# Cross-attention in two blocks of 128 rows on one core: the softmax maxima enter the transposed scores by a 16-row matmul instead of by a DMA into the stacked operand, and the value products are issued four heads at a time

## The reference

```
x = x + L0_xattn(layernorm(x), ctx, ctx)        # this change
x = x + L0_ffn(layernorm(x))                    # one expert product, top-k gates
x = x + L1_xattn(layernorm(x), ctx, mask)
x = x + L1_ffn(layernorm(x))                    # half of the rows, 256 -> 1024 -> 256

def L0_xattn(q, k, v):                          # q, k, v: (16, 128, 256); 8 heads of 16 channels
    qh, kh, vh = (t.reshape(16 * 8, 16, 256) for t in (q, k, v))
    qk = einsum('bdm,bdn->bmn', qh, kh) / sqrt(16)
    return einsum('bmn,bcn->bcm', softmax(qk), vh).reshape(16, 128, 256)
```

## Time and profile before

| what | value |
|---|---|
| time, median of 3 runs | 532.57 us (530.19 to 534.9) |
| span of the profiled execution | 531.3 us |
| PE / DVE / ACT / POOL busy | 361.3 (68%) / 318.5 (60%) / 170.0 (32%) / 94.2 (18%) us |
| DMA moved | 32.87 MB, 62 GB/s in the mean |

### The profile page before, as it was taken

The page is one execution under the profiler, slowest core; times in us unless marked ns, Lnnn a source line. Parts: engine busy times, 40 slices in busy tenths (PEclk is TensorE's granted clock), DMA queues, the critical chain, the costliest instruction groups (busy, mean ns, idle before and its releaser), DMA issues.

```text
span 531.3 us, 7624 instructions
## 1 busy us (share of the span) xinstructions
PE 361.3 (68%) x1872; PEld 207.4 (39%) x1872; DVE 318.5 (60%) x989; ACT 170.0 (32%) x397; POOL 94.2 (18%) x222
## 2 busy tenths in 40 slices
PE   0023494796795795796696799952002699999996
PEld 0011241242342342242243344420002488888885
DVE  6625154376475376376276377546886678887841
ACT  3200151252352252252252344420000125555531
POOL 1101021131131131131130011010001233333310
PEclk9999998699798799699699799985555559999999
DMA  3634363062062062063042000071000000000001
GB/s 104 164 110 103 89 160 74 8 167 68 6 163 71 4 161 72 5 159 73 7 122 73 4 22 1 2 260 57 0 1 0 1 1 11 30 20 20 20 21 41
DMA packets 23763, 32.87 MB, mean 62 GB/s; under 512 B 3466, under 2 KB 21818, under 8 KB 22202
## 3 DMA queue, kind: packets, MB, share of 16 engines
q1 hardware_dynamic: 23706, 32.58, 22.8%
q10 hardware_dynamic: 32, 0.01, 0.0%
HBM read 24.02 MB, written 8.39 MB: 61 GB/s over the span
## 4 chain that ended last, share of the span: by engine, by line
PE 40%; DMA 25%; DVE 15%; issue 7%; SPq 6%; POOL 3%; ACT 2%; DVEq 0%; POOLq 0%; ACTq 0%
DMA q_stack<-neg_max 17%; PE pv_bank L1042 14%; PE t_bank L1248 4%; PE pv_bank L1166 4%; DMA q_parts_dram<-q_parts 4%; PE scoret_bank L1028 4%; DMA q_stack<-q_parts_dram 3%; PE score_bank L1015 3%; SPq L238 3%; PE t_bank L1070 2%; PE score_bank L1229 2%; DMA x_stage<-in_x_dram 1%; PE score_bank L1196 1%; DVE junk L669 1%; DVE equal L669 1%
## 5 line engine op out<-in xcount | busy, mean ns | idle before, releaser
L518 DVE TENSOR_REDUCE row_max<-score_bank 128x2 f32<-128x512 f32 x112 | 75.9, 679 | 121.9 <-PE score_bank L1015 121.7
L1042 PE MATMUL pv_bank<-probs,values_ones 128*32 128x256 f32 x512 | 143.1, 407 | 0.0
L859 ACT ACTIVATE probs<-scoret_bank 128x512 f32<-128x512 f32 x128 | 74.2, 591 | 124.9 <-PE scoret_bank L1028 123.8
L1028 PE MATMUL scoret_bank<-q_stack,k_stack 98*128 98x256 bf16 (+1 forms) x256 | 52.6, 289 | 65.9 <-DMA q_stack<-neg_max 62.9
L1042 PEld LDWEIGHTS pv_bank<-probs,values_ones 128*32 128x32 f32 x512 | 47.7, 114 | 59.0 <-issue 32.5
L1015 PE MATMUL score_bank<-k_stack,q_stack 96*128 (+1 forms) x240 | 49.7, 294 | 24.6 <-DMA q_stack<-q_parts_dram 24.6
L1028 PEld LDWEIGHTS scoret_bank<-q_stack,k_stack 98*128 98x128 bf16 (+1 forms) x256 | 24.7, 102 | 78.3 <-issue 70.1
L358 POOL TENSOR_SCALAR var_eps<-mv 128x1 f32<-128x1 f32 x48 | 9.1, 190 | 192.1 <-DVE mv L554 108.8
L1015 PEld LDWEIGHTS score_bank<-k_stack,q_stack 96*128 (+1 forms) x240 | 17.0, 100 | 66.9 <-issue 27.5
L1166 PE MATMUL pv_bank<-q_stack,k_stack 128*128 (+1 forms) x256 | 36.1, 285 | 0.4 <-ACT q_stack L991 0.4
L1166 PEld LDWEIGHTS pv_bank<-q_stack,k_stack 128*128 128x128 f32 x256 | 33.8, 201 | 1.3 <-issue 0.9
(11 more groups left out here) (182 smaller groups left out, 539.7 us busy)
## 6 DMA issues: line engine op xcount, KB each, us to landing
k_parts_dram<-k_parts SPq DMA_DIRECT2D x24, 128.0 KB
q_parts_dram<-q_parts SPq DMA_DIRECT2D x24, 128.0 KB
k_stack<-k_parts_dram SPq DMA_DIRECT2D x8, 384.0 KB
q_stack<-q_parts_dram SPq DMA_DIRECT2D x8, 384.0 KB
ctx_stage<-in_ctx_dram SPq DMA_DIRECT2D x8, 256.0 KB, 3.2
x_stage<-in_x_dram SPq DMA_DIRECT2D x8, 256.0 KB, 4.2
k_stack<-k_parts_dram SPq DMA_DIRECT2D x8, 256.0 KB
q_stack<-q_parts_dram SPq DMA_DIRECT2D x8, 256.0 KB
```

The costliest lines, as they stand in the source:

```text
L518: dve.tensor_reduce(row_max[:, i, :, h], score_bank[h % 2][:, :].rearrange("p (m n) -> p m n", m=2), AX.X, ALU.max).then_inc(s["max_done"], 1)
L859: act.activation(probs[:, j % 4, :], scoret_bank[j % 2][:, :], ACT.Exp).then_inc(s["exp_done"], 1)
L1028: ins = pe.matmul(scoret_bank[j % 2][:, k * D:(k + 1) * D], k_stack[0:SROWS, slot, h, b_in, k * P:(k + 1) * P], q_stack[0:SROWS, slot, h, ...
L1042: ins = pe.matmul(pv_bank[i][pair * Q:(pair + 1) * Q, odd * D:(odd + 1) * D], values_ones[:, i, k, pair, odd, :], probs[:, j % 4, k * D:(k ...
```

## The change

1. The rows 96 and 97 of the stacks are gone, with the DMA that filled the ones and all `load_neg_max` transfers. Instead DVE negates and splits the maxima before they are transposed (`split_max`, two instructions on 128 x 16 elements in place of one on 8 x 256), one bf16 transpose a half brings both parts of 8 heads to 16 partitions, ACT copies them (`take_neg`) to `neg_rows` (16 x 512), and each half of `scores_t` becomes two matmuls: the 96-row product, and on top of it 16 rows of `neg_rows` against `head_ones`, a constant which is one in the two rows of the head. The semaphore `neg_done` takes the place of `neg_loaded`.
2. The heads are taken in the order 0 2 4 6 1 3 5 7, `probs` has 8 slots, and `values` is called at every fourth step only, for four heads, whose 32-column outputs lie in four different partition groups.
3. `taken_out` and `pick_t`, used in the last layer, lie in a slot of `k_stack`; four small DVE instructions early on make `head_ones`.

```diff
-            def load_neg_max(u, i):
-                wait_apart(sp, s["neg_done"], 2 * u + i + 1)
-                for part in range(2):
-                    sp.dma_start(q_stack[QROWS + part:QROWS + part + 1, u % SLOTS, :, i, :],
-                                 neg_max[:, i, part, :]).then_inc(neg_loaded[i], 16)
...
-            def neg_low(b, i):
+            def split_max(b, i, reused):
+                if reused:
+                    dve.wait_ge(s["max_t"], b - 1)
+                dve.wait_ge(s["max_done"], NH * (b + 1))
+                dve.tensor_scalar(neg_parts[:, i, :, 0, :], row_max[:, i, :, :], -1.0, None,
+                                  ALU.mult).then_inc(s["neg_hi"], 1)
                 dve.wait_ge(s["neg_hi"], b + 1)
-                dve.scalar_tensor_tensor(neg_max[:, i, 1, :], t0_bank[0:NH, 0:D], -1.0, neg_max[:, i, 0, :],
-                                         ALU.mult, ALU.subtract).then_inc(s["neg_done"], 1)
+                dve.scalar_tensor_tensor(neg_parts[:, i, :, 1, :], row_max[:, i, :, :], -1.0, neg_parts[:, i, :, 0, :],
+                                         ALU.mult, ALU.subtract).then_inc(s["neg_split"], 1)
...
+            def take_neg(b, i):
                 act.wait_ge(s["max_t"], b + 1)
-                act.mul(neg_max[:, i, 0, :], t0_bank[0:NH, 0:D], -1.0).then_inc(s["neg_hi"], 1)
+                act.copy(neg_rows[:, i, :], neg_psum).then_inc(s["neg_done"], 1)
...
                 for k in range(2):
-                    ins = pe.matmul(scoret_bank[j % 2][:, k * D:(k + 1) * D],
-                                    k_stack[0:SROWS, slot, h, b_in, k * P:(k + 1) * P],
-                                    q_stack[0:SROWS, slot, h, b_in, :], start=True, stop=True)
+                    pe.matmul(scoret_bank[j % 2][:, k * D:(k + 1) * D],
+                              k_stack[0:QROWS, slot, HEADS[h], b_in, k * P:(k + 1) * P],
+                              q_stack[0:QROWS, slot, HEADS[h], b_in, :], start=True, stop=False)
+                    ins = pe.matmul(scoret_bank[j % 2][:, k * D:(k + 1) * D], head_ones[:, h, :],
+                                    neg_rows[:, b_in, :], start=False, stop=True)
...
-                pe.wait_ge(s["exp_done"], t + 1)
-                pair, odd = h // 2, h % 2
+                pe.wait_ge(s["exp_done"], t + GROUP)
                 for k in range(2):
-                    ins = pe.matmul(pv_bank[i][pair * Q:(pair + 1) * Q, odd * D:(odd + 1) * D],
-                                    values_ones[:, i, k, pair, odd, :], probs[:, j % 4, k * D:(k + 1) * D],
-                                    start=(k == 0), stop=(k == 1))
+                    for pair in range(GROUP):
+                        ins = pe.matmul(pv_bank[i][pair * Q:(pair + 1) * Q, odd * D:(odd + 1) * D],
+                                        values_ones[:, i, k, pair, odd, :],
+                                        probs[:, GROUP * odd + pair, k * D:(k + 1) * D],
+                                        start=(k == 0), stop=(k == 1))
...
-                    values(STEPS * u + j, 2 * u + j // NH, j, first)
+                    if j % GROUP == GROUP - 1:
+                        values(STEPS * u + j + 1 - GROUP, 2 * u + j // NH, j + 1 - GROUP, first)
```

More of the change, by code:

```diff
@@ L31 @@
 QROWS = 6 * C
-SROWS = QROWS + 2
+NR = 2 * NH
+GROUP = NH // 2
+HEADS = [0, 2, 4, 6, 1, 3, 5, 7]
 DIGITS = 15
@@ L78, in build_program @@
         row_max = sb("row_max", [P, 2, 2, NH])
-        neg_max = sb("neg_max", [NH, 2, 2, D], BF16)
+        neg_parts = sb("neg_parts", [P, 2, 2, 2, NH], BF16)
+        neg_rows = sb("neg_rows", [NR, 2, D], BF16)
+        part_head = sb("part_head", [P, 1])
+        head_is = sb("head_is", [P, NH])
+        head_ones = sb("head_ones", [NR, NH, P], BF16)
         low = sb("low", [P, 1])
@@ L512, in _, with maximum @@
             n_consts = k[0]
-            def maximum(step, b, h, i, first_h):
-                if first_h:
-                    dve.wait_ge(s["max_t"], b - 1)
+            def maximum(step, h, i):
                 dve.wait_ge(s["scores_ready"], step + 1)
@@ L573, in unit @@
                     if not last:
-                        maximum(STEPS * (u + 1) + j, 2 * (u + 1) + j // NH, j % NH, j // NH, j % NH == 0)
-                    if j == 1:
-                        neg_low(2 * u + 1, 1)
+                        maximum(STEPS * (u + 1) + j, j % NH, j // NH)
+                    if j == NH - 1 and not last:
+                        split_max(2 * u + 2, 0, True)
+                    if j == STEPS - 1 and not last:
+                        split_max(2 * u + 3, 1, True)
                     if j == 1 and not first:
@@ L590, in unit @@
                         scale_rows(a, 1, second)
-                    if j == 9 and not last:
-                        neg_low(2 * u + 2, 0)
                     if j == 9:
@@ L623, in _ @@
                 first_maxima(0, q)
+            split_max(0, 0, False)
             first_maxima(1, 0)
-            neg_low(0, 0)
             first_maxima(1, 1)
+            split_max(1, 1, False)
             stats_q(2)
@@ L912, in _ @@
             mid_q(1)
-            neg_high(0, 0, 0)
-            act.wait_ge(s["neg_done"], 1)
-            for part in range(2):
-                act.dma_start(q_stack[QROWS + part:QROWS + part + 1, 0, :, 0, :],
-                              neg_max[:, 0, part, :]).then_inc(neg_loaded[0], 16)
+            take_neg(0, 0)
             high_k(2)
@@ L921, in unit @@
                 for j in range(STEPS):
-                    exponential(STEPS * u + j, j, first and j < 4)
+                    exponential(u, j, first and j < NH)
                     if j == 0 and not first:
@@ L927, in unit @@
                     if j == 0:
-                        neg_high(2 * u + 1, u, 1)
+                        take_neg(2 * u + 1, 1)
                     if j == 2 and not first:
@@ L939, in unit @@
                     if j == 9 and not last:
-                        neg_high(2 * u + 2, u + 1, 0)
+                        take_neg(2 * u + 2, 0)
                     if j == 10 and not first:
```

58 lines of the change are left out of this document (27 added, 31 removed).

## The result

| | median of the runs | lowest to highest | ratio to before |
|---|---|---|---|
| before, same chip | 533.29 us | 530.19 to 534.9 | |
| after | 552.19 us | 551.12 to 556.87 | 1.040 (95%: 1.033 to 1.047) |

The change made the kernel 4% slower; forecast were 507 us. The profiled execution after has a span of 550.7 us, 19.4 more than before.

What follows compares the result with a forecast made beforehand. Taken as bound by a loop through DRAM, landing to landing: six loops save 17.5 us, units 6 and 7 fall to 27.5 and 18.4, so values end 25.8 us earlier; span 505.5, forecast 507 us, 8 in 10 within 495 to 519.

Steps and rivals of the forecast that it cites:

- a unit's own work: In the six loops: 31.7 us before and about 28 after, less than the 36.1 us loop, hiding the added matmuls.
- the 17.5 us: Six loops of 36.1 us, 216.6 in all, would bring the last landing to 277.7 instead of 295.2 us.
- Rival (e): TensorE does not regain its upper clock, idling more and draining four times a step: 43 us a unit, 578 us; 4%.
- (c): Tile changes at 16 rows are free, so units 6 and 7 take about 24 and 14 us: 499 us; 8%.
- (b): Values by fours: fp32 passes run in strict order, nine passes a four instead of four, +8.8 us: 516 us; 12%.
- (d): In the loops, q parts follow the landing no sooner, ACT's step at 8 to 10 us: 519 to 531 us; 9%.
- The loop through DRAM: Each unit runs landing to landing: 6.0 to ACT's high part, 3.9, writing 5.6, stack load 20.6, sum 36.1 us.
- (a): The wait for maxima was the transfer's own; loops fall to the unit's work of some 28 us: 458 us; 3%.

Runs made afterwards that it cites:

- full_rows_plus_changes: full_rows with a tiny 16-row, 16-column product of zeros added behind each maxima's product, so four tile changes a step again; 499.4 us, 0.932 to 0.946 of before.
- full_rows: The kernel after with the maxima's product given 96 rows (80 of them zeros) instead of 16, so no tile change there; 486.3 us, 0.911 to 0.925 of before.
- part1_only: The kernel after with values per head in each step and heads in natural order, as before; maxima still by 16-row matmul; 534.4 us, 0.998 to 1.008 of before.

## Why the prediction was wrong, point by point

**The step that failed** is the sentence in part 1 of the change that a unit's own work is "about 28 after (below), less than 36.1, so the added matmuls cost nothing in these loops", and under it the clock: 2.4 GHz from some 5 us after each restart. I took this from the windows before as if it belonged to the engine, but it hung on the mix: there 0.98 of each step of 1.53 us were values per head. The change took three quarters of these away and put in 16-row products with a change of tile on both sides. At 1.2 GHz the unit's own work is 40.7 us, more than the loop, so the end of the loops is TensorE's, and the 17.5 us that were to be gained there are lost. Units 6 and 7 take 36.7 and 28.5 us where 27.5 and 18.4 were forecast.

**Rival (e) took place**, at 4%: it had 43 us a unit and 578 us; measured 40.7 and 552. Its step, 0.44 + 1.36, was sized well (1.71), and so were the values (1.87 for 1.9); its 7 us for the rest of a unit were 5.9, and not all of units 0 to 7 was slow. But the reasons that I gave for it don't hold. TensorE does not "idle more": in the loops the profile shows no wait of it. And that it "drains four times a step" does not do it alone, since full_rows_plus_changes does so too, with a clock of 0.82 from 70 to 230 us. I had priced the changes of tile in microseconds and asked of the clock only whether pauses would pull it down.

The Trainium skill, TensorE: Matmul & The Clock Gate, HAM oscillation, puts a low clock in the middle of a kernel down to idle gaps of the engine. By this rule the kernel after, with 50.00 busy of 50.00 us, would be at 2.4 GHz. The trace disagrees: it is at 0.50.

**What was right**: at 2.4 GHz a matmul of `scores_t` with its change takes 0.21 us (forecast 0.20), so (c) falls, and sixteen records of values take 1.00 us (forecast 1.03, 2.0 by strict order), so (b) falls; ACT's high part comes 66.33 - 62.28 = 4.05 us after the first restart (forecast 6.0), so (d) falls. The loop through DRAM is there once the clock allows it: full_rows has 5.0 to ACT's part, 4.0 to the writing, 5.4 to the stack load and 19.4 to the landing, 33.8 us (forecast 36.1: 6.0, 3.9, 5.6, 20.6). The kernel nearest to my forecast's premise, four changes a step with the clock up, is full_rows_plus_changes: 499 us, inside my range about 507. That is in part luck: its unit 6 starts at 265.2 us (forecast 277.7), and units 6 and 7 take 53.7 us together (forecast 45.9), most of unit 7 at 1.2 GHz; the two errors go against each other. (a), that the wait was the transfer's own, falls: without the transfer full_rows still waits 7 to 9 us for stacks in each loop.

**The range** of 495 to 519 left out (e). (The lower bound of a loop adds up to 34.3 us, not 34.4, which changes nothing.) What the profile could have told me: rows 7 show 2.4 GHz only where values per head fill over half of the time, and no row of before shows TensorE rising on `scores` and `scores_t` alone. That was an unknown with a bound of 2 on every duration of the bounding engine, and I gave it 4%.

## What to carry to other kernels

When an edit takes dense matmuls from TensorE, ask what the clock was resting on (here taking them away alone still gained 5%, and only with the 16-row products as well was it a loss): cost the unit at both levels, and if the slower one exceeds the loop that hides it, that outcome is a main case. A busy share of 100% says nothing of the clock (here it stood at 0.52 in the kernel after and at 1.00 in part1_only); read the spacing of like matmuls. Padding a small contraction to the row count of its neighbours (here 16 to 96 rows, with zeros) saved 66 us at no added time per product (0.11 us from one to the next at 2.4 GHz, in place of 0.21), since it also saves the changes of tile. And where a wait for a DMA is on the chain, look for what its issue hung on: two moved steps of DVE and ACT were worth 21 us, and one load put ahead of another in the same queue cost 33 (499.1 against 465.7).

## What was not expected of the hardware

- TensorE at 1.2 GHz unit after unit while busy all of the time (50.00 of 50.00 us at 0.50), in the kernel with 16-row products and four-group values.
- Nearly the same mix of matmuls at either level: part1_only stood at 1.2 GHz for 34 us of unbroken work and then at 2.4 GHz for 263.
- More full products on TensorE made the same kernel faster: 552.2 to 536.8 us with 256 more records.
- The change of tile costs 0.09 to 0.10 us at 2.4 GHz and, by 311.07 - 310.75 = 0.32 against 0.21 for a product, 0.11 at 1.2 GHz.
- Rows of zeros lift the clock: 80 of the 96 rows in full_rows are zeros, and it goes from 0.52 to 0.83 in the window. Whether other values would lift it as much, no run shows.
- Four fp32 products in four column groups run wholly side by side: sixteen records in 1.00 us, where one head's four take 0.98.
